# 26 of the 56 rows of a convolution's band matrices made in the last steps of the attention stage

## The chip, the cores and the metric

The kernel runs on one core of a Trainium2 chip. Its five engines are TensorE (PE, matmuls; PEld is its weight load), VectorE (DVE), ScalarE (ACT), GpSimd (POOL) and SyncE (SP, which here only issues DMAs). The metric is the time of one execution on the device, in microseconds; lower is better. Times of the kernel before are a median of three runs; the trace is of one more execution.

## What is computed

The input is 8 images of 48 channels and 112 x 112 pixels. Two layers follow each other. The first is a windowed attention (windows of 7 x 7, shifted by 3, three heads) with a feed-forward of 192 units; the second is a depthwise 7 x 7 convolution with a normalised feed-forward:

```
# layer 0, per window of 49 tokens
attn = softmax(q @ k.T * dh**-0.5 + bias);  x = x + roll(attn @ v @ proj_w + proj_b)
x = x + gelu(layernorm(x) @ fc1_w + fc1_b) @ fc2_w + fc2_b
# layer 1
y = depthwise_conv7x7(x) + dw_b;  y = layernorm_over_channels(y)
y = gelu(y @ w1.T + b1);  gx = sqrt(sum over pixels of y*y);  nx = gx / (mean(gx) + eps)
y = grn_g * (y * nx) + grn_b + y;  out = x + y @ w2.T + b2
```

## The kernel before, in words

Three phases follow each other, each a block of its own with a program per engine and a barrier at its end: `attention_phase`, `convolution_phase`, `response_phase`.

**Attention** goes over 64 strips (N = 64; a strip is two bands of 7 image rows, 784 columns on 2 x 49 partitions), unrolled. The order on each engine is written out by hand in `step(s)`: the step for strip s does attention for s, the projection, the first residual and the centring for `prv` = s-1, the second normalisation and the feed-forward for `old` = s-2, and the second residual and the stores for s-3. A call for a strip that doesn't exist issues nothing, so steps 64, 65 and 66 are the run-out, with only the late stages of strips 61, 62 and 63. In PE's step the order is: variance(old), the last weigh of prv, project(prv), centre(prv), fc1(old), fc2(old). `channel_sums` (L856) does centre and variance, L1023 fc1, L1036 and L1042 fc2, L999 project. On DVE: the second residual (L587), the first one (L542), normalise1 (L568), subtract_mean (L553), square (L561), add_bias (L575). On POOL: wrap_columns (L433, L435) of s-3, then x1_low (L450) of prv, low1 (L415) of old, squares_low (L442) of prv. On ACT: log_variance (L712) and root (L718) of old, the gelus (L762), with a table load before and after them. SP stores a finished strip with five DMAs (L336 to L344). `split_taps` on DVE (L672, L675, L678), one part behind each of the run-out's steps, splits the filter taps into a high and a low bf16 piece.

**Convolution.** A channel's 7 x 7 filter is done as products with a band matrix (64 x 64, 7 of them for the 7 columns of taps). All of them lie in `band`, bf16, [128 partitions, 2 pieces, 48 channels, 7, 64 rows o], 86 KB a partition. Row o of every band is a product of `hot` (a one-hot pattern) with `piece`; these are the fills, L1361: 28 of them, each with two rows o, for both pieces and both halves of the partitions, so 8 matmuls a fill. PE alternates between two pairs of PSUM banks a piece and waits for the copies of fill f-2; ACT copies the high piece (L1325), DVE the low one (L1250), as two bf16 side by side at each of 336 places 128 bytes apart. Meanwhile SP loads the input of the first four channels and POOL clears the unused columns of the band. Then ACT copies each channel's band to `band_now` (L1311), DVE makes `x_low` (L1256), and PE convolves (L1378).

**Response** is the feed-forward of layer 1; the change leaves its operations as they are.

## Time and profile before

| | |
|---|---|
| median of 3 runs | 1924.03 us (1917.92 to 1929.37) |
| the profiled execution | 1922.45 us, span 1920.8 us |
| PE / DVE / ACT / POOL busy | 91% / 83% / 80% / 65% of the span |
| instructions | 90622 |
| attention's last dense microseconds | up to about 1290 us |
| run-out of attention | about 1290 to 1333 us |
| band fills | 1333 to 1360 us |
| convolution | 1361 to 1564 us |
| response | about 1576 us to the end |

How to read it: busy is the share of the span in which an engine ran an instruction, over stages with different limits. A row of the time line gives the start, the length of the group, the engine, the line of the kernel, the operation with its tiles and shapes, and in square brackets the idle time before it and what ended that. The granted clock (PEclk) is TensorE's, as a share of full speed: 1.00 is 2.4 GHz, 0.50 is 1.2 GHz.

### The profile page before, as it was taken

Reading aid. Unit: us, or ns where it says so; the run is one execution under the profiler, and the core shown is the slowest. Engines: PE = TensorE matmul, PEld = TensorE weight load, DVE = VectorE, ACT = ScalarE, POOL = GpSimd, SP = SyncE. Lnnn points to the kernel's source line nnn. Section 1 sums busy time; section 2 is a strip of 40 time slices with the busy share of each in tenths; the row PEclk is TensorE's granted clock in tenths of the full one; section 3 lists DMA queues with packets and bytes.
Section 4 is the critical chain, followed back from the end, with each engine's and each line's share of the span. In section 5 each row is a group of like instructions: output and inputs, shape, how many; then the busy total and the mean of one; then the engine's idle time right before and its main releaser. Section 6 shows DMA issues by size and latency. Waiting matters only on the chain. (4 is left out here: it accounts for less than half of the span.)

```text
span 1920.8 us, 90622 instructions
## 1 busy us (share of the span) xinstructions
PE 1741.0 (91%) x38180; PEld 1035.6 (54%) x38180; DVE 1593.1 (83%) x2134; ACT 1536.0 (80%) x3090; POOL 1245.8 (65%) x1048
## 2 busy tenths in 40 slices
PE   5999999999999999999999999996999968998996
PEld 3656656665565666656566566651577743333332
DVE  6899889999999999899989999864777757888883
ACT  3788888888888888888888888884666649888881
POOL 5788888888888888888888888763355540221222
PEclk9999999999999999999999999995899985999998
DMA  4343554434444443444444343423488759999994
GB/s 115 90 114 97 151 132 111 111 98 111 102 117 105 106 115 96 117 100 118 102 111 112 101 115 99 98 57 70 112 215 216 214 145 177 240 253 257 263 256 143
DMA packets 233230, 262.25 MB, mean 137 GB/s; under 512 B 167078, under 2 KB 179910, under 8 KB 232710
## 3 DMA queue, kind: packets, MB, share of 16 engines
q1 hardware_dynamic: 217478, 217.47, 46.8%
q0 software_dynamic: 15360, 39.08, 6.7%
q8 instruction: 304, 4.98, 1.2%
q14 instruction: 88, 0.72, 0.1%
HBM read 160.79 MB, written 80.88 MB: 126 GB/s over the span
## 5 line engine op out<-in xcount | busy, mean ns | idle before, releaser
L425 POOL TENSOR_TENSOR shift<-const_b,qmax 113x588 bf16<-113x588 bf16 x256 | 413.9, 1617 | 219.6 <-DVE qmax L520 219.6
L512 DVE TENSOR_TENSOR Ul<-Uf 113x784 bf16<-113x784 f32 x192 | 260.2, 1381 | 0.0
L520 DVE TENSOR_REDUCE qmax<-ps_s 113x12 f32<-113x588 f32 x256 | 195.4, 763 | 50.6 <-PE ps_s L917 46.8
L1537 POOL DMA_DIRECT2D out_rolled<-r_OUT x128 | 63.8, 503 | 264.3 <-DVE r_OUT L1606 264.3
L1378 PE MATMUL conv_ps<-xin,band_now 64*64 64x448 bf16 x2688 | 202.8, 364 | 2.2 <-DVE x_low L1256 2.2
L731 ACT ACTIVATE P<-ps_t 113x588 f32<-113x588 f32 x256 | 170.0, 664 | 39.0 <-PE ps_t L969 36.6
L724 ACT COPY Uf<-ps_m 113x392 f32<-113x392 f32 x384 | 172.8, 485 | 29.7 <-PE ps_m L882 21.6
L741 ACT COPY V<-ps_t 49x192 f32<-49x192 f32 x512 | 168.8, 330 | 8.8 <-PE ps_t L969 2.4
L984 PEld LDWEIGHTS ps_o<-P,V 113*32 113x32 f32 x6144 | 108.0, 109 | 103.4 <-ACT P L731 52.4
L762 ACT ACTIVATE G<-ps_m 128x392 f32<-128x392 f32 x256 | 113.9, 502 | 46.5 <-PE ps_m L1023 46.2
L984 PE MATMUL ps_o<-P,V 113*32 113x49 f32 x6144 | 141.6, 210 | 8.7 <-DVE O L531 2.7
L415 POOL TENSOR_TENSOR xhl<-xh 113x784 bf16<-113x784 f32 x64 | 146.6, 2291 | 2.4 <-DVE xh L568 2.4
L531 DVE TENSOR_TENSOR O<-ps_o,rden 96x196 f32<-96x196 f32 x256 | 89.5, 349 | 68.3 <-ACT rden L754 68.2
L450 POOL TENSOR_TENSOR xl<-x 113x784 bf16<-113x784 f32 x64 | 140.7, 2198 | 7.3 <-DVE x L542 7.3
L1227 POOL DMA_DIRECT2D y_scratch<-y x96 | 67.9, 707 | 108.9 <-ACT y L1317 102.1
L990 PE MATMUL ps_o<-P,pack 113*32 113x98 f32 x3072 | 134.9, 248 | 0.0
L1378 PE MATMUL conv_ps<-x_low,band_now 64*64 64x448 bf16 x1344 | 133.8, 351 | 0.0
L398 POOL TENSOR_TENSOR t_cen<-XT,t_mean 112x672 f32<-112x672 f32 x64 | 125.1, 1955 | 10.5 <-DVE t_mean L491 10.4
L1643 ACT ACTIVATE r_G<-r_ps_f 128x784 f32<-128x784 f32 x128 | 104.6, 837 | 32.5 <-PE r_ps_f L1696 32.4
L1378 PEld LDWEIGHTS conv_ps<-xin,band_now 64*64 64x64 bf16 x2688 | 102.6, 105 | 34.0 <-issue 3.6
L747 ACT ACTIVATE lden<-ps_o 96x196 f32<-96x196 f32 x256 | 83.2, 325 | 43.7 <-PE ps_o L990 42.2
L407 POOL TENSOR_TENSOR xl<-xh 113x784 bf16<-113x784 f32 x64 | 114.7, 1793 | 2.8 <-DVE xh L506 2.8
(233 smaller groups left out, 5324.2 us busy)
## 6 DMA issues: line engine op xcount, KB each, us to landing
xin<-rows_scratch SPq DMA_DIRECT2D x96, 236.0 KB, 3.7
XT<-x_tokens SPq DMA_DIRECT2D x64, 294.0 KB, 3.5
X<-x_windows SPq DMA_DIRECT2D x128, 147.0 KB, 3.3
RS<-rs_scratch SPq DMA_DIRECT2D x128, 147.0 KB, 3.1
XR<-x_windows SPq DMA_DIRECT2D x128, 147.0 KB, 3.1
x_scratch<-x SPq DMA_DIRECT2D x128, 147.0 KB, 3.4
y_scratch<-y POOLq DMA_DIRECT2D x96, 196.0 KB, 2.8
r_RS<-rs_scratch SPq DMA_DIRECT2D x128, 147.0 KB, 4.3
```

Source lines behind the costliest of these rows:

```text
L398: nc.gpsimd.tensor_tensor(t_cen[:].rearrange("p (t c) -> p t c", c=C), XT[:, s.slot(2), :].rearrange("p (t c) -> p t c", c=C), mean, ALU.s ...
L415: nc.gpsimd.tensor_tensor(xhl1[:], xh1[:], xm1[0], ALU.subtract).then_inc(S["lo1"], 1)
L425: nc.gpsimd.tensor_tensor(shift[:, j % 2], e, m, ALU.mult).then_inc(S["md"], 1)
L450: nc.gpsimd.tensor_tensor(xl1[:], x1[:, r, :], x1m[0][:, r, :], ALU.subtract).then_inc(S["x1_lo"], 1)
L512: nc.vector.tensor_tensor(Ul[:, r, h, :], Uf[:, r, h, :], U[0][:, r, h, :], ALU.subtract).then_inc(S["u_lo"], 1)
L520: nc.vector.tensor_reduce(qmax[:, j % 2, :].rearrange("p (b n) -> p b n", b=2), ps_s[0:R, :, 0:2 * HQ].rearrange("p b (n t) -> p b n t", t ...
L724: nc.scalar.copy(Uf[:, s.slot(2), h, cols_of(b)], bank(("u", h), b)[0:R, 0:HALF]).then_inc(S["u_hi"], 1)
L731: nc.scalar.activation(P[:, j % 2].rearrange("p (b n) h t -> p b n (h t)", b=2), ps_t[0:R, :, 0:2 * SV].rearrange("p b (n c) -> p b n c", ...
L741: nc.scalar.copy(*kept_values(p, j)).then_inc(S["vev"], 1)
L984: mm(ps_out[lo:lo + 2 * DH, at:at + TOK], V[:, j % 2, k, DH * h:DH * h + DH, :], P[:, j % 2, k, h, :], start=True, stop=True)
L990: ins = mm(ps_den[lo:lo + 2 * DH, at:at + 2 * TOK], key_ones[:], P[:, j % 2, 2 * b:2 * b + 2, h, :], start=True, stop=True)
L1378: ins = mm(ps[s][SIDE * k:SIDE * k + SIDE, side, 0:half * IMG], band_now[lo:lo + SIDE, s, w, t, :], part[lo:lo + SIDE, s, half * k:half * ...
```

## The change

1. **Early rows.** Rows o = 0 to 25 of the bands are no longer filled in the convolution's first part, whose fills run from 13 to 27. They are made in attention's run-out, in three parts: 6 rows in step 64 behind project(63), 5 rows in step 65 ahead of fc1(63), 15 rows behind PE's last step. A row has two items, high and low; an item is two matmuls of 336 columns into one of three PSUM banks (both of `ps_t` and `ps_o`, which attention no longer uses), taken in turn, so each item waits for the copy of the third one before it. ACT copies the high items: part 0 behind its table load in step 64, part 1 at the same place in step 65, part 2 at the end. DVE copies the low ones: part 0 in step 64 behind the first residual of 63 and normalise1 of 62, part 1 in step 65 and part 2 in step 66 behind the second residual. One bf16 is written at each of 336 places.
2. **One area.** `band` now lies in `room`, one tile that spans attention and convolution. Thirteen of attention's tiles (XT, t_cen, t_sqr, X, RS, xh0, xl0, swap, swap_l, Uf, Ul, shift and P) are cut out of it too. Y and RS of the response are allocated ahead of attention.
3. **Variance.** variance(63) on PE moves from the front of step 65 into step 64, behind fc1(62) and ahead of fc2(62). It writes to the banks of `ps_s` and also waits for the gelu that empties them.
4. **DVE's order.** In step 65 normalise1(63) moves ahead of the second residual of 62. The three parts of `split_taps` stand together ahead of step 64.

POOL's and SP's programs in attention are not changed.

```diff
--- before.py
+++ after.py
@@ -1,3 +1,4 @@
+import math
 from contextlib import ExitStack
 
...
@@ -161,26 +162,39 @@
-        XT = sb("XT", [ROWS_T, 2, TPR * C])
+        room = later["room"]
+        taken_room = [0]
+
+        def carve(shape, dt=F32):
+            rows_, dims = shape[0], shape[1:]
+            words = math.prod(dims) // (2 if dt == BF16 else 1)
+            at, taken_room[0] = taken_room[0], taken_room[0] + words
+            flat = room[0:rows_, at:at + words]
+            if dt == BF16:
+                flat = flat.bitcast(BF16)
+            names = "abcd"[0:len(dims)]
+            return flat.rearrange(f"p ({' '.join(names)}) -> p {' '.join(names)}", **dict(zip(names, dims)))
+
+        XT = carve([ROWS_T, 2, TPR * C])
-        t_cen = sb("t_cen", [ROWS_T, TPR * C])
-        t_sqr = sb("t_sqr", [ROWS_T, TPR * C])
+        t_cen = carve([ROWS_T, TPR * C])
+        t_sqr = carve([ROWS_T, TPR * C])
...
-        X = sb("X", [R, 2, STRIP])
-        RS = sb("RS", [R, 2, STRIP])
+        X = carve([R, 2, STRIP])
+        RS = carve([R, 2, STRIP])
         XR = sb("XR", [R, 2, STRIP])
-        xh0 = sb("xh0", [R, HRING, STRIP])
-        xl0 = sb("xl0", [R, HRING, STRIP], BF16)
-        swap = sb("swap", [R, 2, HALF])
-        swap_l = sb("swap_l", [R, 2, HALF], BF16)
-        Uf = sb("Uf", [R, 2, UV, STRIP])
-        Ul = sb("Ul", [R, 2, UV, STRIP], BF16)
+        xh0 = carve([R, HRING, STRIP])
+        xl0 = carve([R, HRING, STRIP], BF16)
+        swap = carve([R, 2, HALF])
+        swap_l = carve([R, 2, HALF], BF16)
+        Uf = carve([R, 2, UV, STRIP])
+        Ul = carve([R, 2, UV, STRIP], BF16)
         qmax = sb("qmax", [R, 2, QP * HEADS])
-        shift = sb("shift", [R, 2, QP * HEADS, TOK], BF16)
-        P = sb("P", [R, 2, QP, HEADS, TOK])
+        shift = carve([R, 2, QP * HEADS, TOK], BF16)
+        P = carve([R, 2, QP, HEADS, TOK])
         V = sb("V", [R, 2, QP, C, 2])
         lden = sb("lden", [2 * C, W])
         rden = sb("rden", [2 * C, 2, W])
@@ -257,6 +271,9 @@
         def feature_bank(k, b):
             return ps_s[:, b, :] if k == 1 else bank(("f1", k), b)
 
+        def variance_bank(s, b):
+            return bank("var", b) if s.n < N - 1 else feature_bank(1, b)
+
         def bank(use, b):
             return ps_m[BANKS[use][b]]
 
@@ -272,6 +289,18 @@
...
+
+        EARLY = (6, 5, EARLY_FILLS * 2 - 11)
+
+        def early_bank(w, o):
+            return (ps_t[:, 0], ps_t[:, 1], ps_o[:])[(2 * o + w) % 3][:, 0:C * WS]
+
+        def early_view(w, o):
+            return later["band"][:, w, :, :, o].rearrange("p c t -> p (c t)")
+
+        def early_rows(part):
+            first = sum(EARLY[0:part])
+            return range(first, first + EARLY[part])
 
...
 
@@ -480,6 +509,11 @@
... 
+            def keep_low_bands(part):
+                for o in early_rows(part):
+                    wait(dve, later["low_filled"], o + 1)
+                    nc.vector.tensor_copy(early_view(1, o), early_bank(1, o)).then_inc(later["low_kept"], 1)
+
...
@@ -591,7 +625,13 @@
 
             def step(s):
                 old, prv, nxt, nx2 = s.at(-2), s.at(-1), s.at(1), s.at(2)
+                if old.n == N - 1:
+                    normalise1(old)
                 second_residual(s.at(-3))
+                if old.n == N - 1:
+                    keep_low_bands(1)
+                if s.n == N + 2:
+                    keep_low_bands(2)
                 divide(prv, 2)
                 query_max(s, 2)
                 token_sums(s.at(4))
@@ -600,7 +640,10 @@
                 normalise0(nx2)
                 query_max(s, 3)
                 first_residual(prv)
-                normalise1(old)
+                if old.n < N - 1:
+                    normalise1(old)
+                if prv.n == N - 1:
+                    keep_low_bands(0)
                 divide(s, 0)
                 u_low(nxt, 0)
                 u_low(nxt, 1)
@@ -679,12 +722,18 @@
 
             steps(step, -1, N)
             for part in range(3):
-                step(Strip(0, N + part, N))
                 split_taps(part)
+            for raw in range(N, N + 3):
+                step(Strip(0, raw, N))
 
 
         @block.scalar
         def _(act):
+
+            def keep_high_bands(part):
+                for o in early_rows(part):
+                    wait(act, later["high_filled"], o + 1)
+                    nc.scalar.copy(early_view(0, o), early_bank(0, o)).then_inc(later["high_kept"], 1)
 
...
@@ -709,7 +758,7 @@
                 if s.real:
                     wait(act, S["var"], 2 * s.n + b + 1)
-                    nc.scalar.activation(rs[:, cols_of(b)], bank("var", b)[0:R, 0:HALF], ACT.Ln, scale=1.0 / C,
+                    nc.scalar.activation(rs[:, cols_of(b)], variance_bank(s, b)[0:R, 0:HALF], ACT.Ln, scale=1.0 / C,
                                          bias=eps[:, 0:1]).then_inc(S["ln"], 1)
 
             def root(s):
@@ -791,6 +840,8 @@
                 invert_sums_end(s, 1)
                 if old.real:
                     nc.scalar.preload_act_table_set("gelu_and_others")
+                if s.n >= N:
+                    keep_high_bands(s.n - N)
                 gelu(old, 0, 0)
                 gelu(old, 0, 1)
                 gelu(old, 1, 0)
@@ -811,6 +862,7 @@
...
             steps(step, -1, N + 2)
+            keep_high_bands(2)
 
 
         @block.tensor
@@ -866,7 +918,15 @@
             def variance(s):
                 if s.real:
                     wait(pe, S["sq_lo"], s.n + 1)
-                    channel_sums(1, sqm, "var", s, S["ln"])
+                    if s.n < N - 1:
+                        channel_sums(1, sqm, "var", s, S["ln"])
+                        return
+                    wait(pe, S["ge"], 6 * (s.n - 1) + 4)
+                    for b in range(2):
+                        for m in range(2):
+                            ins = mm(variance_bank(s, b)[0:R, 0:HALF], sum_w[:, 1, :], sqm[m][:, cols_of(b)],
+                                     start=(m == 0), stop=(m == 1))
+                        ins.then_inc(S["var"], 1)
 
...
@@ -1043,6 +1103,18 @@
...
 
+            def early_bands(part):
+                wait(pe, later["split"], 3)
+                for o in early_rows(part):
+                    for w, filled in enumerate((later["high_filled"], later["low_filled"])):
+                        lo, item = 32 * w, 2 * o + w - 3
+                        if item >= 0:
+                            wait(pe, later[("high_kept", "low_kept")[item % 2]], item // 2 + 1)
+                        for side in range(2):
+                            ins = mm(early_bank(w, o)[SIDE * side:SIDE * side + SIDE], later["hot"][lo:lo + WS, o, :],
+                                     later["piece"][w][lo:lo + WS].rearrange("p c t -> p (c t)"), start=True, stop=True)
+                        ins.then_inc(filled, 1)
+
             def step(s):
                 old, prv, nxt = s.at(-2), s.at(-1), s.at(1)
                 before = s.at(-3)
@@ -1055,7 +1127,8 @@
                 query_bias(s, 2)
                 query_scores(s, 2)
                 shift_scores(s, 0)
-                variance(old)
+                if old.n < N - 1:
+                    variance(old)
                 weigh(prv, 3)
                 u_product(nxt, 0)
                 keys_and_values(s, 1)
@@ -1064,6 +1137,10 @@
                 query_scores(s, 3)
                 shift_scores(s, 1)
                 project(prv)
+                if prv.n == N - 1:
+                    early_bands(0)
+                if old.n == N - 1:
+                    early_bands(1)
                 weigh(s, 0)
                 u_product(nxt, 1)
                 keys_and_values(s, 2)
@@ -1080,18 +1157,22 @@
                 shift_scores(s, 3)
                 fc1(old, 1)
                 fc1(old, 2)
+                if prv.n == N - 1:
+                    variance(prv)
                 weigh(s, 2)
                 query_bias(nxt, 1)
                 query_scores(nxt, 1)
                 fc2(old)
 
             steps(step, -1, N + 2)
+            early_bands(2)
 
 
 
 
 
 PIECES = 2
+EARLY_FILLS = 13
 ROWS = 32 * (PIECES - 1) + WS
 BLOCK = IMG // 2
 SEEN = BLOCK + 2 * SHIFT
@@ -1130,7 +1211,7 @@
...
-        band = sb("band", [128, 2, C, WS, SIDE], BF16)
+        band = later["band"]
...
@@ -1245,8 +1326,8 @@
...
 
-            for f in range(FILLS):
-                dve.wait_ge(low_filled, f + 1)
+            for f in range(EARLY_FILLS, FILLS):
+                dve.wait_ge(low_filled, f - EARLY_FILLS + 1)
                 nc.vector.tensor_copy(fill_view(1, f), fill_ps(1, f).rearrange("p o k -> p k o")).then_inc(band_low, 1)
 
             def low(c, s, turn):
@@ -1320,13 +1401,13 @@
...
 
-            for f in range(FILLS):
-                act.wait_ge(high_filled, f + 1)
+            for f in range(EARLY_FILLS, FILLS):
+                act.wait_ge(high_filled, f - EARLY_FILLS + 1)
                 nc.scalar.copy(fill_view(0, f), fill_ps(0, f).rearrange("p o k -> p k o")).then_inc(band_high, 1)
 
             act.wait_ge(band_cleared, 2)
-            act.wait_ge(band_high, FILLS)
-            act.wait_ge(band_low, FILLS)
+            act.wait_ge(band_high, FILLS - EARLY_FILLS)
+            act.wait_ge(band_low, FILLS - EARLY_FILLS)
             for c in range(AHEAD):
                 copy_band(c, c)
             act.wait_ge(bias_made, 4)
@@ -1351,9 +1432,9 @@
             mm = nc.tensor.matmul
             pe.wait_ge(later["split"], 3)
 
-            for f in range(FILLS):
-                wait(pe, band_high, f - 1)
-                wait(pe, band_low, f - 1)
+            for f in range(EARLY_FILLS, FILLS):
+                wait(pe, band_high, f - EARLY_FILLS - 1)
+                wait(pe, band_low, f - EARLY_FILLS - 1)
                 for o in range(PER):
                     for w, filled in enumerate((high_filled, low_filled)):
                         lo = 32 * w
@@ -1362,8 +1443,8 @@
                                      piece[w][lo:lo + WS].rearrange("p c t -> p (c t)"), start=True, stop=True)
                         if o == PER - 1:
                             ins.then_inc(filled, 1)
-            pe.wait_ge(band_high, FILLS)
-            pe.wait_ge(band_low, FILLS)
+            pe.wait_ge(band_high, FILLS - EARLY_FILLS)
+            pe.wait_ge(band_low, FILLS - EARLY_FILLS)
 
             def convolve(c, s, turn):
                 wait(pe, low_made, c + 1)
@@ -1890,6 +1971,9 @@
     return a, c, r
 
 
+ROOM = 21700
+
+
 def program(nc, x_in, x_tokens, packs, out_dram, images):
     scratch = {}
     for name, shape in (("x2_scratch", (images, C, PLANE)), ("rows_scratch", (C, ROWS_IN, images, PAD)),
@@ -1902,22 +1986,26 @@
 
 
         tiles, loads = response_weights(nc, sb, packs[2])
-        later = {name: ctx.enter_context(nc.semaphore("later_" + name)) for name in ("loaded", "split")}
+        later = {name: ctx.enter_context(nc.semaphore("later_" + name))
+                 for name in "loaded split high_filled low_filled high_kept low_kept".split()}
+        for name in ("Y", "RS"):
+            later[name] = sb("r_" + name, [R, 2, STRIP])
         with ExitStack() as inner:
             bands, taps = convolution_weights(
                 nc, lambda name, shape, dt: inner.enter_context(nc.sbuf_tensor(name, shape, dt)),
                 packs[1])
             later["sum_w"] = tiles["sum_w"]
             later["loads"] = taps + loads
-            later.update({name: bands[name] for name in ("taps", "rest", "piece")})
+            later.update({name: bands[name] for name in ("taps", "rest", "piece", "hot")})
+            room = inner.enter_context(nc.sbuf_tensor("room", [128, ROOM], F32))
+            later["room"] = room
+            later["band"] = room[:, 0:C * WS * SIDE].bitcast(BF16).rearrange("p (w c t o) -> p w c t o", w=2, c=C, t=WS)
             attention_phase(nc, x_in, x_tokens, packs[0], scratch["x2_scratch"],
                             scratch["rows_scratch"], scratch["rs0_scratch"], STRIPS * images, later)
-            for name in ("Y", "RS"):
-                later[name] = inner.enter_context(nc.sbuf_tensor("r_" + name, [R, 2, STRIP], F32))
             convolution_phase(nc, bands, tiles, later, scratch["rows_scratch"], scratch["y_scratch"], scratch["rs_scratch"],
                               images)
-            response_phase(nc, tiles, later, scratch["x2_scratch"], scratch["y_scratch"], scratch["rs_scratch"], out_dram,
-                           STRIPS * images)
+        response_phase(nc, tiles, later, scratch["x2_scratch"], scratch["y_scratch"], scratch["rs_scratch"], out_dram,
+                       STRIPS * images)
 
 
 def kernel(**inputs):
```

## Rows read from the trace of the kernel before

**Rows 1.** The page: 40 slices of 48 us; PE busy, granted clock, in tenths.
```profile
PE   5999999999999999999999999996999968998996
PEclk9999999999999999999999999995899985999998
```

**Rows 2.** Stretches: length, busy us of each engine, PEclk, DMA share, GB/s.
```profile
1333.00:1361.00 28.00, 21.34 (x224) 6.27 (x225) 24.77 (x36) 23.68 (x30) 9.57 (x11) 0.50 0.31 71
```

**Rows 3.** Groups by line, 1290 to 1362: shapes, count, busy, mean ns, idle.
```profile
L1361 PE MATMUL conv_ps<-piece,pack_c 7*64 7x336 bf16 x224 | 21.3, 479 | 11.5 <-PEq L105 7.3 <-DVE band L1250 4.3
...
L1325 ACT CAST band<-conv_ps 128x672 bf16<-128x672 f32 x28 | 22.5, 846 | 14.5 <-PE conv_ps L1361 14.5
...
L1250 DVE CAST band<-conv_ps 128x672 bf16<-128x672 f32 x28 | 22.7, 854 | 3.0 <-PE conv_ps L1361 3.0
```

**Rows 4.** Time line of PE and DVE, the end of the fills.
```profile
1357.24 1.54 PE L1361 MATMUL conv_ps<-piece,pack_c 7*64 7x336 bf16 x16 [0.31 <-DVE band L1250]
1361.02 0.59 PE L1378 MATMUL conv_ps<-xin,band_now 64*64 64x448 bf16 x4 [2.23 <-DVE x_low L1256]
...
1358.09 1.62 DVE L1250 CAST band<-conv_ps 128x672 bf16<-128x672 f32 x2 [0.23 <-PE conv_ps L1361]
```

**Rows 5.** Time line of PE, from the last full step through the run-out.
```profile
1288.72 1.54 PE L1036 MATMUL ps_m<-G,pack 128*64 128x392 f32 x8 [0.44 <-ACT G L762]
1290.19 0.89 PE L1042 MATMUL ps_m<-G,pack 64*64 64x392 f32 x8
...
1295.09 2.63 PE L999 MATMUL ps_m<-O,pack 96*113 96x392 f32 x4 [1.55 <-DVE O L531]
1300.67 0.58 PE L856 MATMUL ps_m<-x,sum_w 113*113 113x392 bf16 x1 [2.95 <-POOL xl L450]
...
1306.84 2.88 PE L1036 MATMUL ps_m<-G,pack 128*64 128x392 f32 x8 [1.13 <-ACT G L762]
...
1311.16 0.57 PE L856 MATMUL ps_m<-sq,sum_w 113*113 113x392 bf16 x1
...
1317.11 0.54 PE L1023 MATMUL ps_m<-xh,w_part_h 49*64 49x392 bf16 x4 [4.34 <-POOL xhl L415]
...
1324.32 1.58 PE L1042 MATMUL ps_m<-G,pack 64*64 64x392 f32 x8
1333.17 1.33 PE L1361 MATMUL conv_ps<-piece,pack_c 7*64 7x336 bf16 x16 [7.27 <-PEq L105]
```

**Rows 6.** Time line of DVE in the run-out.
```profile
1291.20 1.04 DVE L587 TENSOR_TENSOR x<-ps_m,x 112x392 f32<-112x392 f32 x2 [4.16 <-issue]
...
1298.31 0.96 DVE L568 TENSOR_TENSOR xh<-xc,rs 113x784 f32<-113x784 f32 x1
...
1326.03 1.04 DVE L587 TENSOR_TENSOR x<-ps_m,x 112x392 f32<-112x392 f32 x2 [10.33 <-issue]
```

**Rows 7.** Time line of POOL in the run-out.
```profile
1304.06 1.75 POOL L442 TENSOR_TENSOR sql<-sq 113x784 bf16<-113x784 f32 x1 [1.99 <-DVE sq L561]
...
1315.37 1.68 POOL L415 TENSOR_TENSOR xhl<-xh 113x784 bf16<-113x784 f32 x1 [2.37 <-DVE xh L568]
```

**Rows 8.** Time lines inside two fills: hand-over from PE to DVE and back.
```profile
1335.03 0.78 PE L1361 MATMUL conv_ps<-piece,pack_c 7*64 7x336 bf16 x8 [0.52 <-DVE band L1250]
...
1335.87 0.86 DVE L1250 CAST band<-conv_ps 128x672 bf16<-128x672 f32 x1 [0.23 <-PE conv_ps L1361]
...
1336.88 0.49 PE L1361 MATMUL conv_ps<-piece,pack_c 7*64 7x336 bf16 x4 [0.32 <-DVE band L1250]
```

**Rows 9.** Stretches of 1 us behind fc2(62); columns as in rows 2.
```profile
1313.00:1314.00 1.00, 0.00 (x0) 0.00 (x0) 0.00 (x0) 0.97 (x2) 0.00 (x0) 1.00 0.08 22
...
1317.00:1318.00 1.00, 0.89 (x12) 0.36 (x12) 0.00 (x0) 0.00 (x0) 0.05 (x1) 0.50 0.38 76
```

**Rows 10.** Two lines: count, ns min/median/max, first and last start.
```profile
L512 DVE TENSOR_TENSOR Ul<-Uf x192: 957/1142/2266, 28.2 to 1270.1; 113x784 bf16<-113x784 f32 x192
...
L731 ACT ACTIVATE P<-ps_t x256: 647/661/677, 35.8 to 1290.4; 113x588 f32<-113x588 f32 x128
```

## The prediction, made before the changed kernel ran

> **What bounds the kernel now.** I read the page first: in which of its 40 slices TensorE (PE) is busy and what clock it was granted [rows 1]. The reader is to see two stages filled to the brim, slices 2 to 27 (attention) and 29 to 32 (convolution, PE at 9 tenths and more), and between them slice 28, about 1297 to 1345 us, in which PE is busy 6 tenths and the granted clock is 0.5. All that the change touches on purpose lies in that dip. The dip in order of time: attention's run-out, in which each engine only finishes the last strips (N is 64, so they are 62 and 63), then a barrier, then the fill of the convolution's bands, then the convolution.
>
> The fill [rows 2 to 4, 8]: 224 matmuls L1361, at half clock throughout (granted 0.50, the 1.2 GHz of its two levels; PE 21.34 of 28 us busy), emptied by 28 copies on ScalarE (ACT, 846 ns) and 28 on VectorE (DVE, 854 ns). From the pair of fills that starts at 1335.03 to the pair that starts at 1357.24 there are 12 pairs in 22.21 us: 1.851 a pair, 0.925 a fill. Both copies of a fill run beside each other; DVE is the later. The fills take 1333.17 to 1359.71 (1358.09 + 1.62), 26.5 us, and the first product of the convolution follows at 1361.02, behind the first x_low. Nothing runs beside the fill that anyone waits for, so a fill less is 0.925 us less.
>
> The run-out [rows 5 to 7] is one chain: project(63) at 1295.09, DVE and POOL, centre(63) 1300.67, fc1(62), fc2(62) from 1306.84 to 1311.2 (2.88 and 1.58 us), variance(63) 1311.16, ACT and DVE, the low half of xhl on POOL 1315.37 to 1317.05, fc1(63) 1317.11, fc2(63) to 1325.90, the residual L587 to 1327.07, POOL, SP's stores, barrier, first fill 1333.17. Two things matter. PE idles 2.95 us before centre and 4.34 before fc1(63). From the end of fc2(63) to the first fill there are 7.3 us in which PE, DVE (but for 1.4 us) and ACT have nothing.
>
> **What goes.** 13 of 28 fills: 13 x 0.925 = **-12.0 us** in the convolution's prologue. The other 15 keep their pace. The prologue gets to the first x_low after 14.5 us instead of 26.5; the loads of xin move with the barrier and keep 14 us for 8 transfers, POOL's clears of the band likewise, and I price both at nothing (if a load were late, each microsecond of it would come back one for one).
>
> **What an early row costs.** A row is two items (a high part that ACT copies, a low part that DVE copies), two matmuls each, over a ring of three PSUM banks instead of four pairs. So item i waits for the copy of item i-3. The loop is: matmul about 0.48 + 0.02 [rows 3], to the copy's start 0.06 (eight matmuls last from 1335.03 to 1335.81, DVE's copy of them starts at 1335.87), the copy, and 0.15 back to PE (that copy ends at 1336.73, the matmul that waited for it starts at 1336.88) [rows 8]. The copy of 336 elements isn't in the trace. From below it is half of the 672-element one, 0.42; from above it is the same 0.85, if it is the count of separate destinations that costs (before, two bf16 lie side by side at each of 336 places; early, one lies at each of 336). Nearest is L587, 392 elements out of PSUM in 0.52 us (1.04 for two, rows 6); 336 at a like rate with its fixed part are 0.46 to 0.48, which I take. Loop: 0.50 + 0.06 + 0.47 + 0.15 = 1.18 us for three items, 0.79 for a row. Laid out item by item from the point at which the first DVE copy may start, n rows end about 0.75 n us later. In the fill a row costs 0.46. An early row is dearer; it pays only where it is hidden.
>
> **Part 0, 6 rows, between project(63) and centre(63).** ACT is free. DVE reaches its low copies only after normalise1(62), 1298.31 + 0.96 = 1299.27 [rows 6]. Items 0 to 3 go out before; item 4 needs DVE's first copy, 1299.27 + 0.48 + 0.15 = 1299.9; 7 more items at 0.33 to 0.39 put the last one at 1302.35. Centre was free to go at 1300.67. Queued behind the waiting PE are centre, fc1(62) and all after: **+1.8 us** on the chain here (+1.3 with the shortest copy, +3.0 with the longest).
>
> **Variance(63) ahead of fc2(62).** sq_lo comes from POOL's L442, 1304.06 to 1305.81 [rows 7]; moved by 1.8 it is 1307.6. PE needs 5.04 us from centre(63) to the end of fc1(62) (1300.67 to 1306.84 less the idle 1.13, rows 5), so that fc1(62) ends at about 1307.5. Variance runs 1307.8 to 1309.4 and fc2(62) behind it to 1313.8 instead of 1311.2. What this buys on ACT and DVE (rs(63) and xh1(63) no longer wait for fc2) is not collected: POOL's order is untouched, wrap_columns(62) stands ahead of low1(63), and it waits for the residual of fc2(62). So fc1(63) follows: 1313.8, residual on DVE 1.1, POOL's two wraps 0.6, low1 1.68 [rows 7], with hand-overs, about 1317.5, against 1317.11. normalise1(63) ahead of the residual on DVE costs nothing, as it is done (about 1313) before fc2(62) is.
>
> **Part 1, 5 rows, between fc2(62) and fc1(63).** The idle 4.34 us is its cover. Its DVE copies start behind the residual, about 1315.0; ten items end on PE at about 1317.4. It and low1 come due together, so this part costs 0 to 0.3, and up to 2 with the long copy. Both parts and the variance together: fc1(63), and so the end of fc2(63), **+0.4 us**.
>
> **Part 2, 15 rows, behind fc2(63).** 30 items. The first DVE copy starts at 1327.07 + 0.4; the last copy ends 11.2 us later, at 1338.7. Its cover, the stores of strip 63, lasted until just before 1333.17. With an estimate of 0.4 for the barrier behind the copies the first fill is at 1339.1 instead of 1333.17: **+5.9 us**, the 0.4 of the run-out within it. With matmuls of 0.32 instead of 0.50 it is +4.3; with the long copy +9.3 before the run-out's own share.
>
> **The rest.** split_taps, three DVE operations moved ahead of step 64, needs under 2.6 us; DVE idled 4.16 us ahead of the residual of strip 61 [rows 6], and that cover is beside PE's full stage, so nothing. If it were gone, at most 2.6 us. SP's queue is unchanged. The tiles of attention in one area are the same operations at other addresses: 0 (see the rivals). Y and RS, allocated earlier, change no instruction.
>
> **Sum.** -12.0 + 5.9 = -6.1 us against the profiled execution's 1922.45 us (span 1920.8), that is 1916.3. The median of the runs before is 1924.03, 1.6 more; against it the sum gives **1917.9 us**, a ratio of 0.997. The terms' own bounds: the row pace -1.8 to +1, the run-out -2 to +1, the barrier 0.3 either way: 1914 to 1921.
>
> **Rival A: the clock comes back in the run-out.** The granted clock was 1.00 (2.4 GHz) in the microsecond from 1313 [rows 9], right after fc2(62) and variance(63) had kept PE busy without a break, and by the time fc1(63) came it was at 0.50 again [rows 9]. Early rows fill the gaps ahead of centre and fc1(63). The Trainium skill ("TensorE: Matmul & The Clock Gate", Part 1) says that sustained activity releases the throttle and idling brings it back; by that rule filling the gaps would pay beyond the rows themselves. That the clock rose behind fc2 agrees. Against it stands the fill [rows 2]: such matmuls, closer together than early ones, stay at 0.50 for 28 us. If it comes nonetheless, fc2(62) gives back 2.0 us (2.88 + 1.58 against 1.54 + 0.89 at full clock, rows 5), fc1(63) and fc2(63) up to 3, part 2's matmuls 1.8, 6.8 together, less about 1.8 that POOL's and DVE's parts of the chain keep: -6.1 - 5 = -11.1, **1912.9 us**.
>
> **Rival B: the narrow copy costs as much as the wide one.** 0.85 us a copy: part 0 puts centre at +3.0, part 1 leaves fc1(63) at +2.8, and part 2 adds its +9.3, 12.1 against 12.0: **1924.1 us**, no gain. For it speaks that the old copy writes at 336 places too, so that its 0.85 us can be read as so much a place. Against it: L587 writes 392 elements in 0.52 us, and 0.52 x 672 / 392 = 0.89 is no less than the 0.854 of DVE's copy [rows 3, 6]; by the element nothing is left to explain. The Trainium skill ("SBUF — State Buffer", Door 1: The DMA port swizzle) says that accesses that leave a 16-byte line pay; every element of an early copy does, as every pair of the old one did, and no row here separates the two.
>
> **Rival C, the other side: the addresses.** XT, X, RS, xh0, the U pairs, shift and P lie elsewhere in SBUF for the whole 1290 us of attention. It decides from 6.1 / 64 = 0.1 us a strip. The price: DVE's L512 takes 957 ns at best, 1142 in the median and 2266 at worst [rows 10], so what goes on beside it matters; one of its three a strip from best to median is 0.185 x 64 = +11.8 us, **1929.6 us**. Against it: the two slots of P lie at two addresses, and L731 stays within 647 to 677 ns over 256 uses [rows 10].
>
> **Chances.** Forecast 0.6; A 0.18; B 0.14; C 0.08. For the range, A and most of B have to be in: 1911.5 to 1925. 0.5% (9.6 us) is about what a measurement of this kernel can tell from no change. Faster by more: most of A and the low edge of the forecast (against a median that moves by some 3 us itself), 0.2. Slower by more: C, most of it, 0.07. The rest, 0.73, within.
>
> **What would show it.** Right, step by step: 120 matmuls of the fill and 104 early ones; first fill at about 1339, 14.5 us to its end; centre(63) near 1302.5; fc1(63) within 1 us of 1317.5; ACT and DVE copies of 336 elements at 0.45 to 0.5, row pace 0.75 in part 2. Wrong: 1.00 in the clock during fc2(62) or fc1(63) (A); copies of 0.8 (B); a first strip of the run-out that begins other than at 1290 +/- 1 (C). The forecast would also fall if the copies of part 2 ended before the stores do.

## The result, and the profile after

The changed kernel takes **1933.8 us** (median of 6 runs, 1930.4 to 1938.1) against 1922.3 us (6 runs, 1914.8 to 1929.4) for the kernel before: 11.5 us slower by the medians, 13 by the ratio, which is 1.0069 [1.0053, 1.0084]. The prediction was 1917.9 us, a gain of 6 us, with a range of 1911.5 to 1925. It was wrong in sign and in size. The profiled execution of the changed kernel took 1932.3 us, its span 1930.4.

The page of the kernel after: PE busy and granted clock, 40 slices of 48 us, to be laid beside [rows 1]. Slices 28 and 29 are both in the dip now (PE 6 and 8 tenths, clock 5 and 7); before, slice 29 had PE at 9 and the clock at 8.

```profile
PE   5899999999999999999999999986899968989996
PEclk9999999999999999999999999985799985999998
```

The time line of PE in the kernel after; what stands in brackets is the idle time ahead and what ended it. It answers to [rows 5]: project(63), two of the early items of part 0, centre(63), fc2(62), fc1(63), the end of fc2(63), the first fill, and the convolution's first product.

```profile
1290.91 1.68 PE L1059 MATMUL ps_m<-O,pack 96*113 96x392 f32 x4 [1.55 <-DVE O L565]
...
1294.77 0.49 PE L1114 MATMUL ps_t<-piece,pack_c 7*64 7x336 bf16 x2 [1.49 <-ACT room L736]
...
1298.08 0.49 PE L1114 MATMUL ps_t<-piece,pack_c 7*64 7x336 bf16 x2 [0.28 <-ACT room L736]
...
1301.63 0.58 PE L908 MATMUL ps_m<-x,sum_w 113*113 113x392 bf16 x1
...
1308.85 2.88 PE L1096 MATMUL ps_m<-G,pack 128*64 128x392 f32 x8
...
1320.13 0.54 PE L1083 MATMUL ps_m<-xh,w_part_h 49*64 49x392 bf16 x4
...
1327.34 1.59 PE L1102 MATMUL ps_m<-G,pack 64*64 64x392 f32 x8
...
1353.92 1.33 PE L1442 MATMUL conv_ps<-piece,pack_c 7*64 7x336 bf16 x16 [2.10 <-PEq L106]
...
1369.89 0.59 PE L1459 MATMUL conv_ps<-xin,band_now 64*64 64x448 bf16 x4 [2.23 <-DVE x_low L1337]
```

PE goes from one matmul of an early item to the wait for a copy, again and again. The first fill comes 25 us behind the end of fc2(63) (1327.34 + 1.59), where it was 7.3 before. What fills those 25 us are the copies. Below are their groups on DVE and on ACT from 1288 to 1354 us (count | busy us, mean ns | idle before them), and two places of DVE's time line, the first copy of part 2 and the last two.

```profile
L515 DVE CAST room<-ps_t 128x336 bf16<-128x336 f32 x18 | 29.5, 1758 | 0.0
L515 DVE CAST room<-ps_o 128x336 bf16<-128x336 f32 x8 | 14.1, 1763 | 0.0
...
L736 ACT CAST room<-ps_t 128x336 bf16<-128x336 f32 x17 | 28.3, 1765 | 4.9 <-PE ps_t L1114 4.8
L736 ACT CAST room<-ps_o 128x336 bf16<-128x336 f32 x9 | 16.5, 1835 | 0.0
```
```profile
1330.01 1.69 DVE L515 CAST room<-ps_o 128x336 bf16<-128x336 f32 x1
...
1350.33 3.26 DVE L515 CAST room<-ps_t 128x336 bf16<-128x336 f32 x2
```

**A copy of 336 elements takes 1.76 us**, twice as long as the old one of 672 (0.85, [rows 3]), not half as long. The 15 of part 2 follow each other on DVE without a gap from 1330.01 to 1353.59: 23.6 us, 1.57 us a row. (One copy's record overlaps the next by up to 0.2 us, so the pace is a little below the mean.)

Both engines write at once for most of this time, and one could ask whether that is what makes a copy slow. ACT's first copy and DVE's first two in the kernel after:

```profile
1293.05 1.68 ACT L736 CAST room<-ps_t 128x336 bf16<-128x336 f32 x1 [0.54 <-PE ps_t L1114]
```
```profile
1294.05 3.20 DVE L515 CAST room<-ps_t 128x336 bf16<-128x336 f32 x2
```

ACT's starts 1.00 us before DVE's. At 0.85 us or less it would have been over by then; it takes 1.68.

To set the traces side by side I count from the start of project(63), since that start itself falls anywhere from 1290.9 to 1295.5 us in these kernels (see e4). Each entry is the start of that line in the time line of PE less the start of project(63); "product" is the first matmul of the convolution, and "prologue" the time from the first fill to it.

| kernel | project(63) starts | centre(63) | fc1(63) | fc2(63) ends | first fill | product | prologue |
|---|---|---|---|---|---|---|---|
| before | 1295.09 | 5.58 | 22.02 | 30.81 | 38.08 | 65.93 | 27.85 |
| after | 1290.91 | 10.72 | 29.22 | 38.02 | 63.01 | 78.98 | 15.97 |
| e1_pairs | 1294.37 | 6.23 | 19.76 | 28.56 | 39.81 | 55.79 | 15.98 |
| e7_pairs_old_order | 1292.64 | 6.2 | 26.5 | 35.3 | 46.5 | 62.5 | 16.0 |
| e3_no_rows | 1295.50 | 4.56 | 17.93 | 26.06 | 33.46 | 61.40 | 27.9 |
| e4_room_only | 1293.24 | 4.53 | 20.72 | 29.4 | 36.7 | 64.6 | 27.9 |

After less before: centre(63) +5.1, fc1(63) +7.2, first fill +24.9, prologue -11.9, the product +13.0 us. The spans of the two traces differ by less, 9.6 us, since project(63) itself starts 4.2 us earlier in this trace of the kernel after; behind the product the two differ by 0.7. One more reservation: project(63) lasts 2.63 us in the trace of before [rows 5] and 1.57 to 1.68 in after, e1, e3, e4 and e7. Against e4, the kernel before with the common area, the product is 14.4 us later in the kernel after.

### The profile page after: what moved, and what is told of

It is laid out like the page before. It is cut to its first block and busy times, and to the rows that moved or that the text cites. A ratio compares the mean times of both kernels' runs of the same rounds, so it can differ in the third digit from the quotient of the medians.

```text
span 1930.4 us, 90637 instructions
## 1 busy us (share of the span) xinstructions
PE 1747.4 (91%) x38180; PEld 1079.1 (56%) x38180; DVE 1627.7 (84%) x2147; ACT 1566.9 (81%) x3103; POOL 1246.2 (65%) x1048
## 5 line engine op out<-in xcount | busy, mean ns | idle before, releaser
L454 POOL TENSOR_TENSOR room<-const_b,qmax 113x588 bf16<-113x588 bf16 x256 | 414.2, 1619 | 216.1 <-DVE qmax L554 216.1
L546 DVE TENSOR_TENSOR room<-room 113x784 bf16<-113x784 f32 x192 | 263.8, 1400 | 0.0
L1001 PE MATMUL ps_t<-room 49*49 49x196 bf16 x6144 | 189.0, 253 | 23.4 <-ACT room L780 14.8
L1001 PEld LDWEIGHTS ps_t<-room 49*49 49x49 bf16 x6144 | 143.3, 101 | 103.2 <-issue 49.1
L780 ACT ACTIVATE room<-ps_t 113x588 f32<-113x588 f32 x256 | 170.0, 664 | 36.3 <-PE ps_t L1029 34.0
L773 ACT COPY room<-ps_m 113x392 f32<-113x392 f32 x384 | 172.8, 485 | 29.7 <-PE ps_m L942 21.6
L1044 PEld LDWEIGHTS ps_o<-room,V 113*32 113x32 f32 x6144 | 107.7, 109 | 102.6 <-ACT room L780 53.0
L1044 PE MATMUL ps_o<-room,V 113*32 113x49 f32 x6144 | 141.1, 210 | 8.2 <-DVE O L565 2.6
L1050 PE MATMUL ps_o<-room,pack 113*32 113x98 f32 x3072 | 134.5, 247 | 0.0
L427 POOL TENSOR_TENSOR room<-room,t_mean 112x672 f32<-112x672 f32 x64 | 126.7, 1980 | 10.5 <-DVE t_mean L525 10.4
```

Of the source, the lines that this page charges most:

```text
L454: nc.gpsimd.tensor_tensor(shift[:, j % 2], e, m, ALU.mult).then_inc(S["md"], 1)
L546: nc.vector.tensor_tensor(Ul[:, r, h, :], Uf[:, r, h, :], U[0][:, r, h, :], ALU.subtract).then_inc(S["u_lo"], 1)
L773: nc.scalar.copy(Uf[:, s.slot(2), h, cols_of(b)], bank(("u", h), b)[0:R, 0:HALF]).then_inc(S["u_hi"], 1)
L780: nc.scalar.activation(P[:, j % 2].rearrange("p (b n) h t -> p b n (h t)", b=2), ps_t[0:R, :, 0:2 * SV].rearrange("p b (n c) -> p b n c", ...
L1001: mm(ps_t[to:to + TOK, b, SV * k:SV * k + SV], token_columns(ws, lo, s, w), U[ms][lo:lo + C + 1, r, :, TOK * w:TOK * w + TOK], start=(k == ...
L1044: mm(ps_out[lo:lo + 2 * DH, at:at + TOK], V[:, j % 2, k, DH * h:DH * h + DH, :], P[:, j % 2, k, h, :], start=True, stop=True)
```

## The experiments

**e1_pairs: the same work, with two neighbouring bf16 written at a time.** An early item is 168 columns of two neighbouring rows o and o+1 instead of 336 of one row. The copy still moves 336 elements out of PSUM, but writes two side by side at 168 places, 128 bytes apart. Four shorter matmuls stand for two. All else is the kernel after.

```diff
         def early_view(w, o):
-            return later["band"][:, w, :, :, o].rearrange("p c t -> p (c t)")
+            lo, k = o // 2 * 2, o % 2
+            return later["band"][:, w, HC * k:HC * k + HC, :, lo:lo + 2].rearrange("p c t o -> p (c t) o")
...
```

What is left out reads the bank in pairs and issues the four matmuls.

> The changed kernel, with only the shape of an early item altered: it is half the columns (168) of two neighbouring rows instead of all 336 columns of one row, so that its copy still has 336 elements in one PSUM bank but writes two bf16 side by side at 168 places. Counts, ring, parts and waits are those of the changed kernel (26 units for 26 rows). In the changed kernel such a copy took 1.69 to 1.76 us instead of my 0.47. Theory 'lone element' (a store of a single 2-byte element that stands alone costs several times one that has its neighbour with it): the copies fall to 0.45 to 0.50 us, a loop of three items to 1.2 us, part 2 to about 11 us, centre(63) to 1.8 us later than before, the first fill to about 6 us later than before, and the kernel to 6 us under the kernel before (ratio 0.997). Theory 'distance' (each place 128 bytes from the last one costs, at 1.69/336 = 5 ns a place): 168 places cost 0.85 us, and the kernel is within 1 us of the kernel before (ratio 1.000). Theory 'addresses' (the common area slows attention or the engines' traffic at large): the copies may fall, but the kernel stays slower than before by 5 us or more.

Measured: 1910.2 us, ratio 0.9945 [0.9927, 0.9963] to the kernel before (1920.3). One edit of the form of the early items turns 0.7% of loss into 0.55% of gain (10 us by the medians). Of the expectations, 'lone element' was right on the copy and the other two are refuted: 168 places cost no 0.85 us, and the common area is still there. The time line of DVE in e1_pairs, the first copy of part 2 and the last, and that of PE, the first fill:

```profile
1324.01 0.50 DVE L521 CAST room<-ps_o 128x336 bf16<-128x336 f32 x1
...
1333.35 0.51 DVE L521 CAST room<-ps_t 128x336 bf16<-128x336 f32 x1 [0.23 <-PE ps_t L1121]
```
```profile
1334.18 1.33 PE L1451 MATMUL conv_ps<-piece,pack_c 7*64 7x336 bf16 x16 [0.93 <-PEq L106]
```

A copy takes 0.50 us, 15 rows take 9.85 us (1324.01 to 1333.86), 0.66 a row. The fill starts 0.32 us behind the last copy; that is the barrier, for which I had estimated 0.4. A part of the pace is the clock. Two stretches of part 2 in e1_pairs, columns as in [rows 2], the clock third from the right:

```profile
1325.00:1326.00 1.00, 0.83 (x16) 0.46 (x16) 0.65 (x2) 0.86 (x3) 0.00 (x0) 1.00 0.31 74
1328.00:1329.00 1.00, 0.91 (x14) 0.33 (x14) 0.88 (x2) 0.48 (x2) 0.00 (x0) 0.50 0.73 180
```

At full clock, up to about 1327, three rows take 1.84 us (DVE's copies of `ps_o` start at 1324.01 and 1325.85); at half clock, later, they take 2.16 (1330.03 to 1332.19).

**e2_forms and e8_steps: what a store costs by its form.** In both, some of the early rows' copies go to spare places in other forms and steps, still 336 elements out of the same PSUM banks. Rows 15 to 23 of the band (e2) or 11 to 19 (e8) are zero instead, which leaves that part of the computation out. So their times, 1926.9 and 1931.1 us in one run each, are not used; the length of the copies is. One edit of each, a 4-byte word every 128 bytes (e2) and a bf16 every 8 words, 32 bytes (e8):

```diff
+                    if o in range(15, 19):
+                        ins = nc.vector.tensor_copy(apart_words(1, o), early_bank(1, o))
...
+                    elif o == 13:
+                        ins = nc.vector.tensor_copy(at_steps(half(1)[:, 0:2688], 7, 8, 2), early_bank(1, o))
```

> The changed kernel with the destinations of part 2's copies altered, each form on a line of its own and on both engines: 4 rows as they are (2-byte elements 128 bytes apart), 4 rows written as 4-byte words 128 bytes apart, 2 rows as 2-byte elements 4 bytes apart, 2 rows as 2-byte elements side by side, 1 row as 2-byte elements 8 bytes apart. Rows 15 to 23 of the bands are left zero, so part of the computation is left out; it is there to time the copies. 'Lone element': the 2-byte forms with gaps take 1.7 us whatever the gap, 4 bytes at 128 bytes and 2 bytes side by side take 0.45 to 0.50. 'Distance': the two forms at 128 bytes take 1.7 us whatever the element, those at 4 and 8 bytes and side by side take about 0.47. If it were the reading side or the cast, all forms would take 1.7, but for the one without a cast.

> The changed kernel with the destinations of nine early rows altered to time a copy of 336 elements by the size of what it writes and the step from one to the next, one form to a line: 2-byte elements at steps of 64, 32 and 16 bytes, 4-byte words at steps of 128, 64, 32, 16 and 8 bytes, 2-byte elements at 128. Rows 11 to 19 of the bands are left zero, so part of the computation is left out. From run e2: 2 bytes at 128, 8, 4 and 2 bytes apart took 1.75, 0.90, 0.53 and 0.44 to 0.51 us, 4 bytes at 128 took 0.76 to 0.82. Theory 'read and write of the memory's line': a copy pays for each line it touches, and a store that doesn't fill a 4-byte word pays twice: 4-byte forms take 0.8 us from a step of 16 or 32 bytes up and 0.45 to 0.5 below, 2-byte forms go from 0.90 at 8 bytes to 1.75 at 16 or 32 and stay there. Theory 'only the distance': each form rises evenly with its step up to 128 bytes.

Groups of DVE's copies in e2_forms. L531 writes 4 bytes every 128; L535 bf16 side by side; L533 bf16 every 4 bytes; L537 bf16 every 8; L539 is the form of the change, bf16 every 128.

```profile
L539 DVE CAST room<-ps_t 128x336 bf16<-128x336 f32 x12 | 19.8, 1747 | 0.1
L531 DVE COPY room<-ps_t 128x336 f32<-128x336 f32 x3 | 2.3, 764 | 0.1
L535 DVE CAST G<-ps_t 128x336 bf16<-128x336 f32 x2 | 1.0, 508 | 0.1
L537 DVE CAST G<-ps_o 128x336 bf16<-128x336 f32 x1 | 0.9, 901 | 0.5 <-PE ps_o L1149 0.5
L533 DVE CAST G<-ps_t 128x336 bf16<-128x336 f32 x1 | 0.5, 531 | 0.1
```

Groups of DVE's copies in e8_steps: bf16 every 64, 32 and 16 bytes (L528, L532, L536), 4 bytes every 16 and 8 (L538, L540).

```profile
L528 DVE CAST room<-ps_o 128x336 bf16<-128x336 f32 x1 | 1.6, 1628 | 0.0
...
L532 DVE CAST room<-ps_t 128x336 bf16<-128x336 f32 x1 | 1.6, 1557 | 0.1
...
L536 DVE CAST G<-ps_t 128x336 bf16<-128x336 f32 x1 | 1.7, 1652 | 0.0
L538 DVE COPY G<-ps_t 128x336 f32<-128x336 f32 x1 | 0.7, 746 | 0.0
L540 DVE COPY G<-ps_o 128x336 f32<-128x336 f32 x1 | 0.5, 509 | 0.0
```

All forms together, us for 336 elements, DVE / ACT; most are a single instruction each:

| step, bytes | 2 | 4 | 8 | 16 | 32 | 64 | 128 |
|---|---|---|---|---|---|---|---|
| bf16 alone | 0.51 / 0.44 | 0.53 / 0.54 | 0.90 / 0.90 | 1.65 / 1.66 | 1.56 / 1.56 | 1.63 / 1.65 | 1.75 / 1.76 |
| 4 bytes | | | 0.51 / 0.46 | 0.75 / 0.94 | 0.77 / 1.06 | 0.90 / 1.08 | 0.76 to 0.82 (both) |

What follows: for lone bf16 the time falls to a half from 16 to 8 bytes, nearly halves again to 4, and doesn't rise above 16. That is the pattern of a charge for each 16-byte stretch that the copy enters, some 4.7 ns (1.57 us / 336), as soon as this exceeds the copy's own 0.5 us. For whole 4-byte words it is about half, on DVE 2.3 ns (0.77 / 336). Two bf16 side by side fit the second price: 672 of them at 336 places in 0.85 us [rows 3], 336 at 168 places in 0.50 (e1). So **two** things cost: a place of its own for each element, and that the element is half a word. It isn't the cast, since the pairs are cast too, nor the reading, which is the same for all forms of a run. For lone bf16 ACT and DVE pay alike; for words 16 to 64 bytes apart ACT takes up to 0.3 us longer (0.94 to 1.08), and nothing here shows why. Why a lone bf16 costs twice a word, these runs don't show either. Neither expectation of e2 holds as it was put: lone bf16 are cheap at a step of 4 bytes and at 8 cost half of what they do at 16, so size and distance both count. That of e8, with the line, holds for bf16, and for words on DVE.

The Trainium skill ("SBUF — State Buffer", Door 1: The DMA port swizzle) describes a line of 16 bytes, and says that accesses which leave it pay, while two in one line are enough for full speed. The flat part from 16 bytes on agrees with the line (1.56 to 1.76 us). Lone bf16 8 bytes apart, two to a line, don't: they take 0.90 us, not 0.5, and the measurement decides. The doubling for lone bf16 is not in that rule either.

**e4_room_only and e3_no_rows: the parts without early rows.** e4 is the kernel before with the common area, and Y and RS allocated early; all its order is that of before, split_taps included. e3 is the kernel after with no early rows: it has the area, the variance ahead of fc2(62), DVE's new order and the earlier split_taps. The edit that takes the rows out stands in both:

```diff
-        EARLY = (6, 5, EARLY_FILLS * 2 - 11)
+        EARLY = (0, 0, 0)
...
-EARLY_FILLS = 13
+EARLY_FILLS = 0
```

> The kernel before with nothing but the common area for attention's tiles and the band, and Y and RS allocated early: all order and all rows as before. If addresses don't matter: ratio 1.000, within 2 us. 'Addresses': slower by 5 us or more. Against run e3 it gives what the variance's move and VectorE's order are worth by themselves.

> The changed kernel without its early rows: all 28 fills are back in the convolution; the common area, the move of the last variance, the new order on VectorE and the earlier split_taps stay. If all of the loss lies in the early copies: within 2 us of the kernel before. By my steps the variance's move alone puts fc2(62) 0.7 us later (1.6 us of variance against the idle 1.13 that it fills in part) and, as GpSimd's order holds xh1's low half behind the residual, gains at most 1.6 us on fc1(63): ratio 0.999 to 1.000. 'Addresses': 5 us or more slower than before, with attention's steady part longer.

Measured: e4 1.0016 [0.9996, 1.0036], e3 0.9985 [0.9966, 1.0004]. The area costs nothing that can be told from zero; by e4's interval it is at most 6.9 us. In the traces project(63) starts at 1293.24 (e4) and 1295.50 (e3), on both sides of before's 1295.09 and after's 1290.91, so attention's length varies by 4.6 us between single traces, and the kernel without the area lies within that. From e4 to e3 the ratio falls by 0.3%, with intervals that overlap; the traces say 3.2 us (64.6 to 61.4), 2.8 of it by fc1(63). PE in e3_no_rows, fc2(62) and fc1(63):

```profile
1306.71 2.14 PE L1096 MATMUL ps_m<-G,pack 128*64 128x392 f32 x8
...
1313.43 0.37 PE L1083 MATMUL ps_m<-xh,w_part_h 49*64 49x392 bf16 x4 [3.77 <-POOL xhl L444]
```

The first half of fc2(62) took 2.88 us before [rows 5] and 2.14 here: the clock comes back while it runs, not behind it as in [rows 9]. The 1.13 us for which PE idled ahead of fc2(62) before [rows 5] are filled with the variance now. And the way from fc2(62)'s end to fc1(63) is 3.8 us (1309.66 to 1313.43) instead of 5.9 (1311.2 to 1317.11 [rows 5]), since ACT and DVE finish with the variance while fc2(62) runs. fc1(63) even starts at full clock (0.37 for a matmul instead of 0.54).

**e7_pairs_old_order: e1 with the variance and normalise1 of 63 both in their old places.**

```diff
-                if old.n < N - 1:
-                    variance(old)
+                variance(old)
...
-                if prv.n == N - 1:
-                    variance(prv)
...
```

> Run e1 (rows in pairs) with the last variance and VectorE's normalise1 in their old places; the early rows and the early split_taps stay. It prices the move beside early rows. Theory 'the variance's move pays' (e3 against e4: ratio 0.9985 against 1.0016, 6 us, with an interval of some 5 us; in their profiles the stretch from the last weigh of strip 63 to the first product of the convolution is 63.8 against 67.0 us): this run is 3 us or more slower than e1. Theory of my prediction (the move costs 0.4 us or gains at most 1.6): within 2 us of e1.

Measured: 1918.7 us, 0.9988 [0.9972, 1.0005], against 0.9945 [0.9927, 0.9963] with the move; in the traces 6.7 us (62.5 to 55.8), all of it between centre and fc1(63) (20.3 us against 13.5). In e7_pairs_old_order, first ACT, the root, the table load and its first copy of part 1; then DVE, its first two copies and what stands behind them all; then POOL:

```profile
1310.75 0.86 ACT L770 ACTIVATE rs<-rs 113x784 f32<-113x784 f32 x1
1311.62 1.28 ACT L845 ACT_TABLE_LOAD   x1
1312.92 0.44 ACT L739 CAST room<-ps_t 128x336 bf16<-128x336 f32 x1
```
```profile
1310.45 0.51 DVE L521 CAST room<-ps_t 128x336 bf16<-128x336 f32 x1 [0.49 <-PE ps_t L1110]
1313.94 0.51 DVE L521 CAST room<-ps_t 128x336 bf16<-128x336 f32 x1 [2.97 <-PE ps_t L1110]
...
1316.53 0.96 DVE L608 TENSOR_TENSOR xh<-xc,rs 113x784 f32<-113x784 f32 x1
```
```profile
1317.57 1.49 POOL L450 TENSOR_TENSOR xhl<-xh 113x784 bf16<-113x784 f32 x1 [7.00 <-DVE xh L608]
```

In the old place ACT has the logarithm and the root of 63 and a table load to do before it can empty part 1's banks, DVE idles 2.97 us between two low copies for want of a bank, and normalise1(63) waits behind all of them. The move of the two is not a small extra: it makes the cover under which part 1 costs nothing. How much belongs to the variance and how much to normalise1 isn't separated.

**e5_six_banks: e1 with six PSUM banks in part 2** instead of three, and **e6_pool_order: e5 with low1(63) ahead of wrap_columns(62)** on POOL.

```diff
-            return (ps_t[:, 0], ps_t[:, 1], ps_o[:])[(2 * o + w) % 3][:, 0:C * WS]
+            item, late = 2 * o + w, 2 * sum(EARLY[0:2])
+            banks = (ps_t[:, 0], ps_t[:, 1], ps_o[:])
+            if item >= late:
+                item, banks = item - late, banks + (ps_s[:, 0], ps_s[:, 1], ps_m[0][:])
+            return banks[item % len(banks)][:, 0:C * WS]
...
```
```diff
+                if old.n == N - 1:
+                    low1(old)
...
-                low1(old)
+                if old.n < N - 1:
+                    low1(old)
```

> Run e1 (rows in pairs) with six PSUM banks instead of three for the items of part 2 (ps_s and one bank of ps_m are free by then), so that a copy no longer waits for the round trip over three banks. Theory 'the ring sets the pace of part 2' (e1: 15 rows in 9.85 us, 0.66 a row, while a copy is busy 0.42 to 0.51): the pace falls to about 0.46 a row, part 2 ends 2.7 us earlier, about with the stores of strip 63, and the kernel is 1.5 to 2.7 us under e1, ratio to the kernel before 0.993. Rival: the stores of strip 63 or the copies themselves end no earlier, and nothing moves (0.9945).

> Run e5 with GpSimd's order altered in step 65: low1 of strip 63 ahead of wrap_columns of strip 62, which my prediction named as what keeps the moved variance from paying. If that order were still the limit, fc1(63) would begin up to 1.5 us earlier and the kernel would be 1.5 us under e5. I expect less, 0 to 0.5 us: the two-matmul items of part 1 hold TensorE until about the same time (in e1 the last one ends at 1314.2, low1 at 1314.0).

Measured: e5 1909.0 us, 0.9941 [0.9919, 0.9963], e6 1912.3 us, 0.9948 [0.9929, 0.9967]; neither differs from e1's 0.9945 by more than the intervals. In e5_six_banks: the last DVE copy, SP's last store, PE's first fill, and the line of DMA issues from 1319 to 1334 us that has that store (KB, us from issue to landing), last the same line of the kernel before.

```profile
1328.80 0.50 DVE L525 CAST room<-ps_m 128x336 bf16<-128x336 f32 x1
```
```profile
1326.56 0.46 SPq L383 DMA_DIRECT2D rows_scratch<-x  x1
```
```profile
1330.57 1.33 PE L1459 MATMUL conv_ps<-piece,pack_c 7*64 7x336 bf16 x16 [1.97 <-PEq L106]
```
```profile
rows_scratch<-x SPq DMA_DIRECT2D x1, 66.4 KB, 3.5
```
```profile
rows_scratch<-x SPq DMA_DIRECT2D x1, 66.4 KB, 2.2
```

The copies follow each other at 0.415 us (1328.39 and 1328.80 are two starts), and the last ends at 1329.30. But the first fill waits until 1330.57: the last store of strip 63 lands at 1326.56 + 3.5 = 1330.06, and the barrier follows 0.5 later. With six banks the rows hide wholly behind the stores, and what is late next is the stores. This store takes 3.5 and 3.6 us to land in the two kernels with six banks (e5, e6), and 2.2 to 2.4 in the eight others; what slows it isn't shown. At 2.2 it would have landed before the last copy ended. From the end of fc2(63) to the first fill it is 8.65 us in e5, against 11.25 in e1 and 7.3 before. Of these 2.6 us, 1.1 are left in the trace's product (54.7 against 55.8), because fc1(63) came 1.5 later in e5, whose project(63) took 2.85 us instead of 1.57. The expected 1.5 to 2.7 us are not confirmed by the times: by the ratios, 0.9941 against 0.9945, e5 is 0.8 us ahead, well inside the intervals. As for e6, its trace is 1.1 us shorter than e5's from project(63) to the product, which its time doesn't confirm; no gain is shown.

## Why the prediction was wrong, point by point

**What an early row costs: the step that failed.** Its term "the copy" was 0.47 us, with bounds of 0.42 and 0.85; it measured 1.57 to 1.76. I took the price of L587 per element, a copy that writes its elements side by side, and for the upper bound the copy of 672, whose bf16 come in pairs. Neither row has lone bf16 apart, and the bound rested on "the count of separate destinations", which is one half of what costs. No row of the kernel before showed the form in question. Then a bound is only the price of another form, and should not have closed the range at 1925. The term was off by a factor of 3.7 (1.75 against 0.47). The loop over three banks, in which it stood, then didn't even set the pace: with 1.75 it gives 2.46 us for three items, 1.64 a row, but DVE's copies follow each other without a gap at 1.57, so DVE's own time is the limit. Where the loop does set it, in e1, it was priced too high: 0.79 a row predicted, 0.66 measured, 0.61 at full clock and 0.72 at half.

**Part 0**: +1.8 predicted, +5.1 in the trace. The mechanism (centre queued behind items that wait for copies) stands; the size is the copy. In e1, where a copy costs what I had taken, it is +0.65 against before. That is partly luck: project(63) took 2.63 us before [rows 5] and 1.57 in e1, e3 and e4. Against e3, with the same project, part 0 costs 6.23 - 4.56 = 1.7 us, as predicted; against e3 the slow copies of the kernel after cost 6.2.

**Variance(63) and part 1**: fc1(63) +0.4 predicted, +7.2 in the trace, of which 5.1 are part 0's. The other 2.1 are the sum of two: part 1, whose cover was too short for ten slow copies, and the gain of the variance's move. From centre to fc1(63) the kernel after takes 18.5 us and e3, which has the move and no rows, 13.4: part 1 costs 5.1, where I had up to 2 with the long copy. With copies of 0.5 us (e1) fc1(63) is 2.3 us *earlier* than before, not 0.4 later. From centre to fc1(63), e1 takes 13.5 us and e3, without rows, 13.4: part 1 costs 0.2 there, as predicted. What I missed is the size of the move's gain. I had 15.0 us from centre to fc1(63) (1302.5 to 1317.5); of the 1.5 us between that and 13.5, fc2(62) gives 0.9 (1307.27 to 1310.80, 3.5 us, against 4.4), since it ends at full clock, and low1 0.2, with 1.49 us where it took 1.68 [rows 7]; where the remaining 0.4 come from stays open. That POOL's order holds the rest back, the reason for "not collected", was not confirmed by e6: its undoing brought nothing measurable. And I had not seen that part 1 needs the move (e7).

**Part 2**: I had 11.2 us for 15 rows; it took 23.6 (and 9.85 in e1). First fill +5.9 predicted, +24.9 in the trace: 7.2 from the run-out, and 17.7 from here. The 12.4 us by which part 2 itself was longer than forecast are 15 x (1.57 - 0.75) = 12.3. In e1 it was shorter than forecast by 1.35, in part because the clock was full for its first rows.

**What goes**: -12.0 predicted, -11.9 measured. The fills' pace, the loads of xin behind the barrier and POOL's clears were judged rightly.

**The sum**, term by term: 24.9 - 11.9 = +13.0 instead of 5.9 - 12.0 = -6.1. With the copy that I had assumed (e1) the kernel gains 10.1 us, in the medians and in the traces up to the product: first fill +1.7, prologue -11.9. Forecast for that case was -6.1; the 4 us between are fc1(63) (2.7) and part 2 (11.2 against 9.85).

**Rival A, the clock**: in the kernel after it helped little, as fc2(62) took 4.2 us instead of 4.4. A stretch of 1 us of the kernel after just behind fc2(62), among the early items of part 1, and one in fc1(63) (columns as in [rows 2], the clock third from the right):

```profile
1313.00:1314.00 1.00, 0.45 (x10) 0.11 (x6) 0.82 (x2) 0.65 (x1) 0.00 (x0) 1.00 0.00 0
1320.00:1321.00 1.00, 1.00 (x14) 0.36 (x12) 1.00 (x2) 1.00 (x1) 0.00 (x0) 0.50 0.00 0
```

The same picture as [rows 9]: full clock just behind fc2(62), half clock in fc1(63), here behind items that come 0.8 us apart. In e1 and e3 a part of the effect is there; PE in e1_pairs, fc2(62) and fc1(63):

```profile
1307.27 2.71 PE L1102 MATMUL ps_m<-G,pack 128*64 128x392 f32 x8
1309.91 0.89 PE L1108 MATMUL ps_m<-G,pack 64*64 64x392 f32 x8
...
1314.13 0.54 PE L1089 MATMUL ps_m<-xh,w_part_h 49*64 49x392 bf16 x4
```

Its second half takes 0.89 us, the full-clock value of [rows 5], instead of 1.58; fc1(63) is at half clock again. The rows in the gaps are not what brings this: e3 has none and shows most of it. How much of it is the variance's move, the traces don't settle: with the move, fc2(62) lasts 2.95 us (e3), 3.5 (e1), 3.8 (e5) and 4.2 (after); in the old place 4.4 (before, e4) and 3.8 (e7). In fc2(62) it is 0 to 1.5 us either way, and in e1 some of part 2 on top (three rows in 1.84 us at full clock, 2.16 at half), not the 6.8 of this rival. So its -11.1 and the -10.1 of e1 agree by accident.

**Rival B, the copy as dear as the wide one**, had the right place and half the price. **Rival C, the addresses**: nothing that e4 can tell from zero, with 6.9 us as the end of its interval against the 11.8 of the rival; and in e1, which has the area, the stages priced here add up to the whole of the measured gain.

## What to carry to other kernels

Before work is moved into another form, price the store by its destination: element size, and how many separate 16-byte stretches it enters. A copy of half the elements can cost twice the time if pairs become singles, and another cut of the same work (two neighbours at a time) gets it back. And an upper bound taken from "the nearest row" bounds nothing if that row has another form; then the range has to stay open on that side.
